# FiLM products of a token tile inside the sparse attention, one context buffer per layout, the input norm on GpSimd, biases as row products

## The reference, cut to what matters

```python
Q, K = x_text @ Wq, x_vision @ Wk                    # 4 heads of 32
topv, topi = top_k(Q K^T / sqrt(32), 32)             # sparse attention: 32 of 1601 keys
attn_mean = zeros.set(topi, softmax(topv)).mean(heads)
c_t = (attn_mean @ (x_vision @ Wv)) * text_mask      # 64 x 512 for a batch
x = layernorm(x_text) * g_norm_in + b_norm_in
scale_in, shift_in = split(c_t @ W_film_in + b_film_in)
x = x * (1 + mod_gate * scale_in) + mod_gate * shift_in
y = s4d(x)                                           # a long convolution over 64 tokens, by a Fourier transform
scale_out, shift_out = split(c_t @ W_film_out + b_film_out)
xt = x_text + y * (1 + mod_gate * scale_out) + mod_gate * shift_out
xt = xt + gelu(layernorm(xt) @ W1 + b1) @ W2 + b2
out = layernorm(xt) * g_norm_out + b_norm_out        # added to x
```

## Time and profile before

| | us |
|---|---|
| median of 3 runs | 2322.35 (2321.62 to 2323.28) |
| the profiled execution, its own time | 2323.49 |
| its span, first to last instruction | 2321.7 |
| TensorE busy | 2116.7 (91%) |
| VectorE busy | 1002.7 (43%) |
| ScalarE busy | 699.7 (30%) |
| GpSimd busy | 409.2 (18%) |

### The profile page before, as it was taken

How to read it: one execution, slowest core, us unless ns; L and a number is a source line. 1 busy time by engine, 2 the same in 40 slices (tenths; PEclk the granted TensorE clock), 3 DMA queues, 4 the chain that set the end, 5 groups by cost and what they waited for, 6 DMA issues and landing times. The chain is left out here.

```text
span 2321.7 us, 26085 instructions
## 1 busy us (share of the span) xinstructions
PE 2116.7 (91%) x9802; PEld 1229.8 (53%) x9802; DVE 1002.7 (43%) x2019; ACT 699.7 (30%) x1382; POOL 409.2 (18%) x468
## 2 busy tenths in 40 slices
PE   7989999999999998899999997778599987899999
PEld 3545555555555544544444443333233444899998
DVE  6564655646556403420000016999763046412120
ACT  2444544545445411321111114555301112111111
POOL 0000000000000001079888511222100000000010
PEclk9999999999999998899999999898799988899999
DMA  6102121221212223377888757342250100766652
GB/s 217 41 20 84 39 74 46 69 82 45 72 48 64 93 70 154 116 298 300 312 312 316 289 182 251 126 155 68 71 231 19 42 9 14 305 241 229 240 212 79
DMA packets 130925, 327.12 MB, mean 141 GB/s; under 512 B 39617, under 2 KB 88801, under 8 KB 111474
## 3 DMA queue, kind: packets, MB, share of 16 engines
q1 hardware_dynamic: 98368, 293.59, 35.2%
q10 hardware_dynamic: 29730, 23.29, 3.1%
q0 software_dynamic: 2704, 8.59, 1.1%
HBM read 303.40 MB, written 20.91 MB: 140 GB/s over the span
## 5 line engine op out<-in xcount | busy, mean ns | idle before, releaser
L876 PE MATMUL a_mix<-a_xn,a_probs_T 128*128 128x384 f32 (+1 forms) x832 | 313.2, 494 | 14.9 <-issue 9.9
L805 PE MATMUL a_sc<-a_wk_centred,a_ctx_T 128*128 128x512 f32 x624 | 287.5, 597 | 2.3 <-DVE a_keys L463 2.3
L1936 PE MATMUL c_gate_up<-bc_w_wide,c_h_rows 128*128 128x512 f32 x480 | 210.9, 592 | 0.0
L876 PEld LDWEIGHTS a_mix<-a_xn,a_probs_T 128*128 128x128 f32 (+1 forms) x832 | 145.6, 191 | 120.7 <-issue 73.1
L805 PEld LDWEIGHTS a_sc<-a_wk_centred,a_ctx_T 128*128 128x128 f32 x624 | 117.4, 191 | 125.7 <-issue 104.6
L1840 DVE TENSOR_TENSOR c_hidden<-c_silu,c_gate_up 128x512 f32<-128x512 f32 x38 | 26.1, 688 | 360.0 <-PE c_gate_up L1936 360.0
L1936 PEld LDWEIGHTS c_gate_up<-bc_w_wide,c_h_rows 128*128 128x128 f32 x480 | 90.1, 190 | 108.1 <-issue 108.1
L2391 PE MATMUL f_ring<-f_picked_T,f_w 128*128 128x160 f32 x1024 | 143.5, 300 | 0.0
L2406 PE MATMUL f_ring<-f_hidden,f_w 128*128 128x160 f32 x1024 | 141.4, 300 | 0.8 <-ACT f_hidden L2281 0.8
L2406 PEld LDWEIGHTS f_ring<-f_hidden,f_w 128*128 128x128 f32 x1024 | 139.3, 190 | 1.4 <-ACT f_hidden L2281 1.2
L2391 PEld LDWEIGHTS f_ring<-f_picked_T,f_w 128*128 128x128 f32 x1024 | 139.9, 190 | 0.2
(11 more groups left out here) (535 smaller groups left out, 3229.6 us busy)
## 6 DMA issues: line engine op xcount, KB each, us to landing
bc_w_wide<-in_L_ffn_W SPq DMA_DIRECT2D x64, 1024.0 KB, 5.3
f_w<-in_L_ffn_W SPq DMA_DIRECT2D x32, 2048.0 KB, 8.7
c_w_down<-in_L_ffn_W SPq DMA_DIRECT2D x34, 1024.0 KB, 7.2
a_ctx_T<-in_ctx_T SPq DMA_DIRECT2D x48, 384.0 KB, 3.5
a_xn<-in_ctx SPq DMA_DIRECT2D x24, 768.0 KB, 7.2
d_context<-in_ctx SPq DMA_DIRECT2D x8, 2304.0 KB
d_context_T<-in_ctx_T SPq DMA_DIRECT2D x12, 768.0 KB, 7.0
cd_context_T<-in_ctx_T SPq DMA_DIRECT2D x9, 768.0 KB, 7.7
```

What stands on the lines that cost most here:

```text
L805: last = pe.matmul(key_bank(b, t), ctx_T[:, n % AHEAD, k, cols], wk_centred[:, k, :], start=(k == 0), stop=(k == KC - 1))
L876: ins = pe.matmul(mix[:, 0:DC], probs_T[0:m, t, p * P:(p + 1) * P], xn[0:m, b % 2, t, :], start=(t == 0), stop=(t == CT - 1))
L1936: last = pe.matmul(gate_up[2 * (u % 2) + part][:], h[:, k, :], w_wide[:, i % WIDE_RING, k, :], start=(k == 0), stop=(k == KD - 1))
```

## The change

- In d2 TensorE also makes the film products of the token tiles 0, 1 and 2 (inner) and 0 and 1 (outer), by the table `FILMS_AT`, at the end of a round's list. The outer products of tile 2 and all of tile 3 stay in d3. ScalarE copies each out of PSUM (`take_film`), GpSimd masks the tokens and applies the inner scale and shift.
- The lists of a round are put in another order: TensorE does score(b+2), average(b), keys(b+3), turn_average(b), blend(b), films(b); ScalarE does exponentials(b,1), the film copies of b-1, put_scores(b+2), put_shares(b), exponentials(b+1,0), put_averages(b), put_keys(b+3), put_mean(b), put_mix(b). After round 6 it takes that round's films at once, ahead of exponentials(7,1).
- `context` and `context_T` have one buffer each. A chunk of `context_T` is loaded once the keys of the batch before have read it, `context` once the blend before is done.
- The statistics of the input norm are taken by VectorE in d2, the rest of the norm, gain and bias by GpSimd there. The small weights and the film weights are loaded at the start of d2.
- The film biases, gated by GpSimd on four single rows, enter each product as one more matmul of 32 rows with ones. In d3 `gated`, `each` and two of `finish`'s four additions are gone; GpSimd adds `hn`, `b2` and `b_norm_out`.
- The film weights live in a stage of their own (`df`), which ends after the attention that follows.

```diff
@@ xattn1_context: SyncE
             def load_turned(b):
-                par = b % 2
-                if b >= 2:
-                    sp.wait_ge(keys_full, NC * (b - 1))
                 for c, (lo, hi) in enumerate(CHUNKS):
-                    sp.dma_start(context_T[par][:, :, lo:hi], ...)
+                    sp.wait_ge(keys_full, NC * (b - 1) + c + 1)
+                    sp.dma_start(context_T[:, :, lo:hi], d["ctx_T"][b][:, :, lo:hi]).then_inc(context_T_in[c], 16)
             def load_context(b):
-                if b >= 2:
-                    sp.wait_ge(mix_full, b - 1)
+                if b:
+                    sp.wait_ge(mix_full, b)
...
             load_turned(1)
             load_context(0)
+            early.load(sp, d)
+            films.load(sp, d)
             load_turned(2)
-            load_context(1)
             load_turned(3)
-            load_turned(4)
-            for b in range(2, NB):
+            for b in range(1, NB):
                 load_context(b)
                 if b + 3 < NB:
                     load_turned(b + 3)
-            early.load(sp, d)
@@ GpSimd
+            films.clear(pool)
+            pool.wait_ge(q_full, 1)
+            pool.wait_ge(second.inverted, 1)
+            pool.wait_ge(early.v_in, early.v_count)
+            for t in range(NT):
+                own.did(pool.tensor_scalar(xin[:, t, :], g.hn[:, t, :], second.mv[:, t, 0:1], second.rstd[:, t:t + 1],
+                                           ALU.subtract, ALU.mult))
+            ...                                        # 4 products with g_norm_in, 4 additions of b_norm_in
+            films.gate(pool, early.vecs)
+            for b in range(NB):
+                to_shares(b, 0)
+                for kind, t in FILMS_AT.get(b, ()):
+                    if kind == "value":
+                        mask_tokens(t)
+                if b < NB - 1:
+                    to_shares(b, 1)
+                for what in FILMS_AT.get(b - 1, ()):
+                    if what in STAGED:
+                        modulate(what)
+            mask_tokens(NT - 1)
@@ ScalarE
+            second.on_scalar(act, g.eps[:])
...
             for b in range(NB):
                 exponentials(b, 1)
-                if 1 <= b and b + 2 < NB:
-                    put_keys(b + 2)
+                if b < NB - 1:
+                    for what in FILMS_AT.get(b - 1, ()):
+                        take_film(what)
+                if b + 2 < NB:
+                    put_scores(b + 2)
                 if b < NB - 1:
                     put_shares(b)
+                    exponentials(b + 1, 0)
                 put_averages(b)
+                if b + 3 < NB:
+                    put_keys(b + 3)
                 put_mean(b)
                 if b < NB - 1:
-                    exponentials(b + 1, 0)
                     put_mix(b)
-                if b + 2 < NB:
-                    put_scores(b + 2)
+                if b == NB - 2:
+                    for what in FILMS_AT[b]:
+                        take_film(what)
             put_mix(NB - 1)
@@ TensorE
+        FILMS_AT = {2: (("value", 0), ("in scale", 0)),
+                    3: (("in shift", 0),),
+                    4: (("value", 1), ("in scale", 1)),
+                    5: (("in shift", 1), ("out scale", 0), ("out shift", 0)),
+                    6: (("value", 2), ("in scale", 2), ("in shift", 2), ("out scale", 1), ("out shift", 1))}
             for b in range(NB):
-                average(b)
-                blend(b)
                 if b + 2 < NB:
                     score(b + 2)
+                average(b)
                 if b + 3 < NB:
                     keys(b + 3)
+                turn_average(b)
+                blend(b)
+                for what in FILMS_AT.get(b, ()):
+                    film(what)
@@ class Films
+    def product(self, pe, out, value, i, j):
+        r = slice(32 * (2 * i + j), 32 * (2 * i + j) + 32)
+        w = (self.w_in, self.w_out)[i]
+        pe.matmul(out, self.ones[r, :].to_broadcast([32, P]), self.rows[r, :], start=True, stop=False, ...)
+        for k in range(KD):
+            last = pe.matmul(out, value[:, k, :], w[:, k, j * D:(j + 1) * D], start=False, stop=(k == KD - 1), ...)
@@ film_and_mlp: TensorE
-            film(0, False)
-            film(1, False)
+            pe.wait_ge(value_ready, 1)
+            for j in range(2):
+                films.product(pe, place("in", j)[:], value_T, 0, j).then_inc(full("in", j), 1)
             transform(0)
-            film(2, False)
             transform(1)
-            film(3, False)
+            film_out(2)
             transform(2)
-            film(0, True)
             transform(3)
-            film(1, True)
-            transform_back(0)
-            transform_back(1)
-            film(2, True)
-            transform_back(2)
-            transform_back(3)
-            film(3, True)
+            film_out(3)
+            for t in range(NT):
+                transform_back(t)
@@ film_and_mlp: VectorE (masks, norm, gains, gated biases and modulate(t) go; of modulate only tile 3 stays)
             def finish(t):
-                ...                                    # 4 additions and products, two of them waiting for the film
                 dve.wait_ge(signal_full, t + 1)
+                if t >= 2:
+                    wait_out(dve, "out", t, 0)
+                dve.wait_ge(outer_ready, t + 1)
+                own.did(dve.tensor_tensor(rest[:, t, :], outer[:, t, 0, :], y[t][:], ALU.mult))
+                own.wait()
+                own.did(dve.tensor_tensor(xt[:, t, :], rest[:, t, :], outer[:, t, 1, :], ALU.add))
+                own.wait()
@@ film_and_mlp: GpSimd (new stream)
+            for t in range(NT):
+                if t >= 2:
+                    wait_out(pool, "out", t, 1)
+                pool.tensor_tensor(outer[:, t, 1, :], outer[:, t, 1, :], g.hn[:, t, :], ALU.add).then_inc(outer_ready, 1)
+            pool.wait_ge(long_in, 16 * len(long))
+            for t in range(NT):
+                pool.wait_ge(mlp_normed, t + 1)
+                pool.tensor_tensor(xt[:, t, :], xt[:, t, :], long["b2"][:], ALU.add).then_inc(biased, 1)
+            for t in range(NT):
+                pool.tensor_tensor(g.x[:, t, :], g.x[:, t, :], long["b_norm_out"][:], ALU.add).then_inc(x_biased, 1)
```

395 lines of the change are left out of this document (235 added, 160 removed).

## The result

| | before | after |
|---|---|---|
| median of 20 runs each | 2322.47 us (2315.79 to 2325.3) | 2324.11 us (2322.59 to 2329.13) |
| the profiled execution, its own time | 2323.49 | 2323.82 |
| its span | 2321.7 | 2322.1 |
| mean granted clock | 0.959 | 0.966 |

The ratio after to before is 1.0015, with a 95% interval of 1.0009 to 1.0021. The medians differ by 1.6 us and the means by 3.3, to the slower side; both are inside what I had called no change. The forecast was 2315.0, that is 7.5 us faster.

A forecast was written before the change was run, and what follows sets the result against it. VectorE's picks bound d2, TensorE d3's film phase; moving products under the picks starts the MLP 8.4 us earlier, less 0.8 for a barrier: 7.6, giving 2315 us. Own range 2309 to 2320, outer 2304 to 2327; faster 0.57.

The forecast's parts named there:

- `waves` lands in 8 us: Start of d3: the Fourier matrices' load lands after 8 us, ends 3 and 9.8.
- my first rival: d3's front goes better, with waves after 3 us, no locks and cheaper row products: 2305 us, chance 0.15.
- Rounds with films: d2 from round 2's end: A3 to A6, average starts of rounds 3 to 6, at 1558.3, 1588.5, 1623.6, 1650.6.
- the third rival: Slower: each of four rounds A3 to A6 is x longer, gain 7.6 - 4x; half-clock averages, x = 4.3: 2332; chance 0.15.
- 33 of 54.5 us hidden: d2: of 54.5 us of film work put in, 33 lie hidden and 21.5 show at its end.
- The order costs nothing: d2 rounds: the new order of the lists by itself adds 0 us.
- the cost of a film piece: TensorE in d2 and d3: a film product takes 4.4 us, its bias row 0.88 of that; a value piece 3.5.
- Last picks 1 to 2 us later: Sign at d2's end: VectorE's last picks end 1 to 2 us later than at 1664.1.
- The rest of d3's front: d3 up to the MLP's first product: 64.6 us in all, 8 of them for waves, the MLP starting 8.4 earlier.
- The lock: d3: VectorE's passes lengthened beside GpSimd by their shared ports, 2.5 us, ends 0 and 3.8.
- The fourth rival: d2: with single context buffers the pair's load takes 28 us, keys 6.3 late in rounds 1 and 2: 2321, chance 0.05.
- The second: d3's front goes worse, by late waves (1.8), locks (1.3), a later VectorE end and 2 us of handshakes: 2321, chance 0.20.

The follow-up runs named there:

- e10: Changed kernel with the MLP's first weights (4 MB) requested only once the Fourier matrices have landed: 2311.07 us, ratio 0.9958 to the kernel before.
- e1: Changed kernel with the Fourier matrices loaded in round 6 of d2, not at the start of d3: 2312.64 us, ratio 0.9959 to the kernel before.
- e4: Kernel before with only the new order of TensorE's and ScalarE's lists, no film product moved: 2321.80 us, ratio 0.9999 to the kernel before.
- e2: Changed kernel without the sixteen bias row products, the film biases left out of the computation: 2313.64 us, ratio 0.9963 to the kernel before.
- e5: Changed kernel with ScalarE's share copies, from round 3 on, ahead of the last film copy and score copies: 2322.17 us, ratio 1.0002 to the kernel before.
- e6: Changed kernel with the value product between the blend's and its turning products, its copy ahead of the exponentials: 2319.69 us, ratio 0.9992 to the kernel before.
- e7: Changed kernel with each f32 bias row split into two bf16 row products: 2317.32 us, ratio 0.9978 to the kernel before.
- e8: Changed kernel with early matrices, shares first, value product inside the blend and bf16 bias rows together: 2302.40 us, ratio 0.9916 to the kernel before.
- e9: Kernel with all four repairs, plus ScalarE's average copies ahead of the next exponentials in rounds 5 and 6: 2295.32 us, ratio 0.9893 to the kernel before.
- e3: Changed kernel with tile 1's two outer film products moved from round 6 to before d3's wait for the matrices: 2313.39 us, ratio 0.9965 to the kernel before.

## Why the prediction was wrong

Times here are by the axis of the kernel before. Counted from VectorE's first pick it lies 3.76 us behind that of the profile after. The sum missed by 7.5 us up to d3 and by 6.2 in d3's front. Two of its steps failed: the landing of `waves`, and the pace of TensorE's products in the rounds with films.

- **`waves` lands in 8 us (a step that failed).** It took 13.5, beyond the upper end of 9.8 that I had from the earlier trace rows. I read that row as slowed by two broadcasts of 512 KB, and went down to 8 because they are gone. But these were requested behind `waves`. SyncE's large loads, which I left out, stood beside it in the kernel before too; their requests, and the landing of the first:

```profile
1680.88 0.33 SPq L3168 DMA_DIRECT2D d_w_in_film<-in_L_xattn_W_film_in  x1
1680.89 0.36 ACTq L3308 DMA_DIRECT2D d_waves<-in_waves  x1
1681.27 0.42 SPq L3169 DMA_DIRECT2D d_w_out_film<-in_L_xattn_W_film_out  x1
1681.74 0.43 SPq L3170 DMA_DIRECT2D h_room<-in_L_xattn_W  x1
...
d_w_in_film<-in_L_xattn_W_film_in SPq DMA_DIRECT2D x1, 2048.0 KB, 9.6
```

There the first load on SyncE's queue was 2 MB and landed in 9.6 us, `waves` in 9.8. In the changed kernel the first is W1 with 4 MB, and `waves` took 13.5; with W1 held back it took 2.6 (e10). So the cause of the row was read wrong, and the time went up where I had it go down. Whether the size of the load ahead sets the time was not tested by itself. I had written against my first rival that W1's 4 MB start in the same moment, and left the sum at 8. Idleness and the slow products behind it took 13.8 us (e1, e10), of which the forecast held 6.0 (3.2 of idleness, 1.5 and 1.3 of slow clock). These 7.8 are more than the miss of the front, 70.8 us where I had 64.6: the rest of it went 1.6 better than my sum.
- **Rounds with films, the chain from A3 to A6, the starts of the averages of rounds 3 to 6 (the other step that failed).** The mechanism was right: 1558.3, 1588.5, 1623.6 and 1650.6 were forecast, 1560.5, 1590.4, 1628.4 and 1657.3 came. What failed are the sizes. I had averages of 3.4 us, products at full pace, and a clock of 1.00 in the windows of rounds 3 to 6; it was 0.99, 0.92, 0.94 and 1.00. The average of round 2 started 1.4 late by the order (e4) and took 5.98; of both together 2.2 reached A3. Between A4 and A5 2.9 were added, with an average of 4.68 and an inner product of 5.40, and between A5 and A6 1.9, with an inner product of 5.37; I had 3.5 for each of these products. No run here takes only these slow products out, so their share is read from the rows. By A6 it is 6.7 us, the third rival with x of 1.7, which had named the averages at half clock. The wait of 1.87 for the shares is no miss: from a product's end to the next average it took 6.1 us, as forecast.
- **33 of 54.5 us hidden.** 27 were: exponentials(7,1) came 27.9 us later where I had 21.5. The forecast already had TensorE late from round 2 on; these are the 6 us that it lacked. e2, e5, e6 and e7 show that rows and handshakes on that chain count nearly in full, until the shortened chain meets the picks in rounds 5 and 6.
- **The order costs nothing, the cost of a film piece.** Right for the order at the end of the stage (e4). A product is 4.68 us, not 4.4: the bias row takes 1.05, where I had 0.88 as the upper end. What I drew there from the Trainium skill's section "LDWEIGHTS" is said of the load of the weights, not of the product. Sixteen rows are 2.7 us more than forecast. The sum had charged them, but whether they had to be there never came up, though they are work that did not exist before. e2 prices them at 14.7 us of the stretch, about twice the whole gain that I had forecast.
- **Last picks 1 to 2 us later.** They came 7.2 later: VectorE stood 2.98 and 1.29 us for exponentials, and one TENSOR_SCALAR took 2.93 us (row above) where GpSimd's subtraction ran from 1657.04 to 1660.07 of the profile after; its like at 1689.12, with GpSimd idle, took 0.25. The Trainium skill, "SBUF — State Buffer", section "SBUF: two separate sides", lets one of the two block for a whole instruction; this row agrees. It cost little, since the picks were no longer the bound at the end.
- **The rest of d3's front.** The lock took 2.2 us against 2.5 (two sums of 1.33 and 1.27 for 0.69, one normalising pass of 1.52 for 0.55), and from the last sum to the MLP it took 5.9 us against 6.0. The pass of 1.52 lies within these 5.9. GpSimd's early norm took longer than costed, 8.26 us for four passes where I had 4, and stayed hidden. The fourth rival is out: the keys of rounds 1 and 2 did not wait for a load. The one such wait, 4.33 us, came at 1435.55 of the profile after, ahead of the rounds.

The sum: 7.5 us missed up to d3, 6.2 in its front, 13.7 together, less 1.7 behind the MLP's start, where a barrier charged with 0.8 did not show and 0.9 went the other way, which is no more than that part varies. So 12 us, for a gain of 7.6 forecast and 4.2 lost in the stretch. The prediction said that it would be wrong if d3's front took over 72 us or over 30 us showed at the end of d2; it came within a hair of both, 70.8 and 28.8. The second and the third rival came true at once, each in part. My forecast had them only one at a time. The measured 2324 lies within my outer range of 2304 to 2327, but only because that held the rivals; the forecast itself, faster with a chance of 0.57, did not come.

What stays open: how much each slow product in the rounds costs, and why the clock falls there without an idle stretch as long as those above. That the medians seem to gain less than the stretches is for the most part how they were measured: by their ratios to the kernel before, e1, e7, e8 and e9 gain 13.0, 8.6, 23.0 and 28.3 us on the changed kernel, and by the stretch 13.8, 7.5, 23.5 and 30.6, within the intervals.

## What to carry to other kernels

When work is moved beneath another engine's pace, find the first round in which the moved work makes its engine late. What is added from there on is no longer hidden, handshakes of 2 us are nearly full price, and the gain of each repair lasts only until the old bound is met again. Price a small load by the large ones that are requested in the same moment. Before taking its row from another kernel, list what was requested beside it there. Count an idle stretch of TensorE with the slow products behind it.

## What the runs showed of the chip

- A load of 256 KB landed in 2.6 us alone (e10), in 13.5 (the changed kernel) and 13.4 (e3) beside one of 4 MB that another engine requested, and in 9.8 (the kernel before) beside loads of 2, 2 and 4 MB, the first of which itself landed in 9.6.
- 8.79 us of TensorE idleness were followed by 11.69 us of products that take 6.80 in e1, without the idleness; the window from 1706 to 1731 has a granted clock of 0.67. In e8 an idle stretch of 4.50 us was followed by a blend of 6.34 us for 4.70, at 0.69.
- A row product of 32x512 in f32 costs 1.02 to 1.05 us from start to start, and two in bf16 0.52.
- GpSimd's TENSOR_SCALAR of 128x512 with two operands per partition took 2.07 us (four in 8.26), longer than its TENSOR_TENSOR of the same size (1.24 to 1.27), while VectorE's picks ran beside both.
